# Attention on one core: score matmuls of 32 rows on a packed key tile, and the causal mask of the maximum pass added in PSUM by a matmul

## What is computed

```
scores = jnp.einsum('bhqd,bhkd->bhqk', q, k)
causal = jnp.tril(jnp.ones((t, t), bool))
scores = jnp.where(causal, scores, -jnp.inf)
attn = jax.nn.softmax(scores / np.sqrt(HEAD_DIM).astype(np.float32), axis=-1)
ctx = jnp.einsum('bhqk,bhkd->bhqd', attn, v)
```

## Time and profile before

| what | before |
|---|---|
| median of 3 runs | 1316.02 us (1314.12 to 1316.12) |
| span of the profiled execution | 1311.0 us |
| PE / DVE / ACT / POOL busy | 1194.1 / 1044.4 / 723.5 / 66.6 us |
| units L1204, score matmuls L1164, values L1184 | 1280, 1280 and 2560 matmuls |
| maxima L1314 and L1320 on VectorE | 768 and 512 |

### The profile page before, as it was taken

How to read it: one execution, slowest core, us unless ns; L and a number is a source line. 1 busy time by engine, 2 the same in 40 slices (tenths; PEclk the granted TensorE clock), 3 DMA queues, 4 the chain that set the end, 5 groups by cost and what they waited for, 6 DMA issues and landing times.

```text
span 1311.0 us, 21446 instructions
## 1 busy us (share of the span) xinstructions
PE 1194.1 (91%) x7781; PEld 510.1 (39%) x7781; DVE 1044.4 (80%) x3015; ACT 723.5 (55%) x861; POOL 66.6 (5%) x64
## 2 busy tenths in 40 slices
PE   1999958999999999999699979599999999999997
PEld 1455533333333333334455537233333333333336
DVE  8976588999999887875447567799999989878764
ACT  1322115566777777777332224156667777777773
POOL 5111010000000000000101000100000000000000
PEclk9999979999999999999799989799999999999999
DMA  4100142000000000000000000510000000000001
GB/s 147 34 1 1 39 131 58 2 1 2 2 1 1 2 1 2 1 1 2 1 0 1 1 1 25 154 48 2 2 1 2 2 1 1 2 1 2 2 2 33
DMA packets 23510, 23.26 MB, mean 18 GB/s; under 512 B 3134, under 2 KB 21220, under 8 KB 23404
## 3 DMA queue, kind: packets, MB, share of 16 engines
q1 hardware_dynamic: 22252, 18.73, 4.9%
q0 software_dynamic: 1152, 3.15, 0.9%
HBM read 13.20 MB, written 8.39 MB: 16 GB/s over the span
## 4 chain that ended last, share of the span: by engine, by line
PE 70%; DVE 22%; issue 4%; ACT 2%; DMA 1%; SPq 0%; DVEq 0%; ACTq 0%
PE psum L1184 18%; PE psum L1204 17%; PE psum L1164 14%; PE psum L442 9%; DVE part_max L1314 8%; PE psum L466 2%; PE psum L903 2%; PE psum L1171 2%; DVE junk L1320 2%; DVE xn L167 1%; DVE norm_v L150 1%; PE psum L1224 1%; PE psum L918 1%; DVE norm_stats L141 1%; PE psum L427 1%
## 5 line engine op out<-in xcount | busy, mean ns | idle before, releaser
L1275 ACT ACTIVATE hidden<-psum,exp_scale 128x1024 f32<-128x1024 f32 (+3 forms) x640 | 597.7, 984 | 258.9 <-PE psum L1164 137.3
L1314 DVE TENSOR_REDUCE part_max<-psum 128x1 f32<-128x512 f32 x768 | 492.1, 686 | 59.1 <-PE psum L1204 53.9
L1204 PE MATMUL psum<-k_slots,q_slots 128*128 128x512 f16 (+3 forms) x1280 | 401.2, 356 | 34.2 <-DVE part_max L1314 12.2
L1164 PE MATMUL psum<-q_slots,k_slots 128*128 128x512 f16 (+3 forms) x1280 | 330.9, 348 | 6.3 <-ACT hidden L1275 3.5
L1184 PE MATMUL psum<-hidden,v_aug 128*9 128x512 f32 (+3 forms) x2560 | 293.7, 531 | 0.1
L1320 DVE CUSTOM_DVE_ANT_0 junk<-psum,causal_add 128x384 bf16<-128x384 f32 (+3 forms) x512 | 230.6, 488 | 49.0 <-PE psum L1204 45.9
L1204 PEld LDWEIGHTS psum<-k_slots,q_slots 128*128 128x128 f16 x1280 | 114.5, 97 | 361.1 <-DVE part_max L1314 177.5
L442 PE MATMUL psum<-parts,w_parts 128*128 128x512 f16 x768 | 180.4, 387 | 1.9 <-DVE parts L843 1.9
L1164 PEld LDWEIGHTS psum<-q_slots,k_slots 128*128 128x128 f16 x1280 | 118.3, 98 | 97.8 <-ACT hidden L1275 13.9
L442 PEld LDWEIGHTS psum<-parts,w_parts 128*128 128x128 f16 x768 | 73.7, 99 | 83.1 <-issue 6.8
L586 ACT CAST parts<-psum 128x512 f16<-128x512 f32 x64 | 37.2, 588 | 107.2 <-PE psum L427 107.2
(11 more groups left out here) (170 smaller groups left out, 730.5 us busy)
## 6 DMA issues: line engine op xcount, KB each, us to landing
q_slots<-q_rows SPq DMA_DIRECT2D x8, 512.0 KB, 3.7
k_slots<-k_rows POOLq DMA_DIRECT2D x24, 128.0 KB, 4.1
q_rows<-parts SPq DMA_DIRECT2D x18, 128.0 KB, 2.7
k_rows<-parts SPq DMA_DIRECT2D x18, 128.0 KB, 2.4
q_slots<-in_L_ffn_W_dram SPq DMA_DIRECT2D x2, 1024.0 KB, 6.5
k_slots<-k_rows SPq DMA_DIRECT2D x8, 128.0 KB, 3.9
q_slots<-nm_parts SPq DMA_DIRECT2D x64, 4.0 KB
out_dram<-x_res SPq DMA_DIRECT2D x4, 256.0 KB, 2.3
```

The lines of the kernel that those rows point to most:

```text
L1164: last = pe.matmul(psum[:, S_BANKS + 2 * (tile % 2) + par, off:CH], k_slots[:, G * g + 2 * pr + par, j * P:(j + 1) * P], q_slots[:, g, c * ...
L1204: last = pe.matmul(psum[:, bank, 0:w], q_slots[:, g, qb * P:(qb + 1) * P], k_slots[:, G * g + h, kc * CH:kc * CH + w], start=True, stop=True)
L1275: act.activation(probs[:, tile % NP, :, off:CH], psum[:, bank:bank + 2, off:CH], ACT.Exp, scale=exp_scale[:, layer:layer + 1]).then_inc(ex ...
L1314: dve.tensor_reduce(dst, psum[:, bank, :], axis=AX.X, op=ALU.max).then_inc(ring_read, 1)
```

## The change

1. `k_slots` is packed like `q_slots`: [128, 4, 2048], four heads in the 128 rows, no zeros beside them. Score matmuls and units use the 32 rows of their head alone (`rows_of(h)`), in both operands.
2. VectorE takes plain maxima of all units. The mask of a diagonal unit is added in PSUM by a matmul of `later_keys` and `ident_bf` (128 x 128 rows and columns) on the unit's last 128 columns (`mask_of`). `ring_items` takes a stretch of ring items in groups of at most three: scores of the diagonal units first, then their masks, and only a mask counts up `ring_full`. In a layer there are 170 such groups: 14 in the opening (8 of them of three units), 100 in turns with a full quad (8 of three), 56 in turns with a quad on the diagonal (2 of three).
3. `causal_add` and `junk` are gone. Keys are loaded by one DMA for a chunk, not four. POOL clears one plane of `k_slots` in place of the whole tile.

The masks of the score pass (now L1165) stay matmuls of 128 rows.

```diff
-        k_slots = sb("k_slots", [P, H, T], F16)
+        k_slots = sb("k_slots", [P, NG, T], F16)
...
-                    pool.memset(k_slots[:, :, :].rearrange("p h t -> p (h t)").bitcast(I32), 0).then_inc(slots_set, 1)
-                    pool.wait_ge(slots_set, 1)
+                    pool.memset(k_slots[:, 1, :].bitcast(I32), 0).then_inc(slots_set, 1)
...
-            def load_k_rows(engine, n, h):
+            def load_rows(engine, slots, m, n):
 
                 cols = slice(n * CH, (n + 1) * CH)
-                return engine.dma_start(k_slots[SLOT * h:SLOT * (h + 1), h::G, cols],
-                                        slot_dram[1].rearrange("(g h) i d t -> h (i d) g t", h=G)[h, :, :, cols])
+                return engine.dma_start(slots[:, :, cols],
+                                        slot_dram[m].rearrange("(g h) i d t -> (h i d) g t", h=G)[:, :, cols])
+
+            def rows_of(h):
+                return slice(SLOT * h, SLOT * (h + 1))
...
                     for par in range(2):
+                        rows = rows_of(2 * pr + par)
                         last = pe.matmul(psum[:, S_BANKS + 2 * (tile % 2) + par, off:CH],
-                                         k_slots[:, G * g + 2 * pr + par, j * P:(j + 1) * P],
-                                         q_slots[:, g, c * CH + off:(c + 1) * CH],
+                                         k_slots[rows, g, j * P:(j + 1) * P],
+                                         q_slots[rows, g, c * CH + off:(c + 1) * CH],
                                          start=True, stop=q not in diagonal)
...
-                        last = pe.matmul(psum[:, bank, 0:w], q_slots[:, g, qb * P:(qb + 1) * P],
-                                         k_slots[:, G * g + h, kc * CH:kc * CH + w], start=True, stop=True)
+                        last = pe.matmul(psum[:, bank, 0:w], q_slots[rows_of(h), g, qb * P:(qb + 1) * P],
+                                         k_slots[rows_of(h), g, kc * CH:kc * CH + w], start=True, stop=kc < c)
+                        if kc == c:
+                            return
...
+                def mask_of(item):
+
+                    (_, c), i, kc, _ = item[1]
+                    pe.matmul(psum[:, RING_BANKS + ring_no[item] % RING, i * P:(i + 1) * P], later_keys[:, :],
+                              ident_bf[:, :], start=False, stop=True).then_inc(ring_full, 1)
+
+                def ring_items(items):
+
+                    for first in range(0, len(items), RING):
+                        some = items[first:first + RING]
+                        masked = []
+                        for item in some:
+                            on_diagonal = item[0] == "scores" and item[1][2] == item[1][0][1]
+                            if not on_diagonal:
+                                for before in masked:
+                                    mask_of(before)
+                                masked = []
+                            ring_item(item)
+                            if on_diagonal:
+                                masked.append(item)
+                        for item in masked:
+                            mask_of(item)
...
-                                dve.tensor_tensor_reduce(out=junk[:, n % 2, 0:w], in0=psum[:, bank, 0:w],
-                                                         in1=causal_add[:, CH - w:CH], scale=1.0,
-                                                         scalar=-3.0e38, op0=ALU.add, op1=ALU.max,
-                                                         accum_out=dst).then_inc(ring_read, 1)
-                                junk_used[n % 2] = n + 1
+                            w = CH if kc < s[1] else (i + 1) * P
+                            dve.tensor_reduce(dst, psum[:, bank, 0:w], axis=AX.X, op=ALU.max).then_inc(ring_read, 1)
...
-                    for h in range(G):
-                        load_k_rows(pool, proj.order[n], h).then_inc(k_landed[proj.order[n] - 1], 16)
+                    load_rows(pool, k_slots, 1, proj.order[n]).then_inc(k_landed[proj.order[n] - 1], 16)
...
-                        for h in range(G):
-                            load_k_rows(sp, c, h).then_inc(q_landed[c], 16)
+                        load_rows(sp, k_slots, 1, c).then_inc(q_landed[c], 16)
```

More of the change, by code:

```diff
@@ L1248, in _ @@
                         score_tile(q, 0)
[L1249 to L1250 removed]
+                    ring_items(items[cuts[0]:cuts[1]])
                     if q:
                         score_tile(q, 1)
[L1253 to L1254 removed]
+                    ring_items(items[cuts[1]:cuts[2]])
                     if previous:
                         values(previous)
[L1257 to L1258 removed]
+                    ring_items(items[cuts[2]:cuts[3]])
                     previous = q
```

34 lines of the change are left out of this document (6 added, 28 removed).

## The result

| what | before | after |
|---|---|---|
| median | 1315.89 us (1314.12 to 1316.12, 4 runs) | 1432.88 us (1427.92 to 1443.11, 4 runs) |
| ratio | 1 | 1.0909, 95% interval 1.0862 to 1.0956 |
| the profiled execution: time, span | span 1311.0 us | 1427.92 us, span 1426.0 us |
| mean granted clock of the span | 0.975 | 0.850 |
| time at half clock, 2 x (1 - clock) x span | 66 us | 428 us |

What follows compares the result with a forecast made beforehand. PE was taken to bound plain turns, VectorE only 0.23 us behind. Terms summed to +10.3 us a layer, +20.6 for both, less 1.5 for loads: +19 on 1316, so 1335 us, range 1303 to 1366.

Steps and rivals of the forecast that it cites:

- The granted clock is taken as now.: Whole kernel: the forecast time assumed PE's granted clock stays as in the profile before, 1.00 in the attention stretches.
- The rival that named it: Granted clock falls to half over a tenth of 320 turns because of small PE stops: +48 us, 1383 us; chance 0.04.
- A change of shape: PE switching between matmuls of different rows x columns: 0.096 us each, 550 more changes, 53 us of PE a layer.
- the rival of a cheaper change: Changes to 32-row tiles cost less than priced, deciding at 0.077 us; at 0.055 the kernel is faster, 1290 us; chance 0.22.
- the serial one: Rival: 32-row tiles run one after the other, so the pairs save nothing: 1448 us; chance 0.06.
- Item 2: Turns with a full quad and no diagonal unit (41 a layer): side-by-side pairs save 9.1 us a layer.
- Item 5: Turns with a quad on the diagonal and diagonal units (31 a layer): +11 us a layer, between 0 and 17.8.
- Item 3: Turns with a full quad and diagonal units (55 a layer): pairs against shape changes and masks, +3 us a layer.
- Item 4: Turns with a quad on the diagonal, no diagonal unit (33 a layer): +1 us a layer, between -4 and +5.5.
- Item 1, the opening: Opening of 32 diagonal units: VectorE idles 0.48 to 0.63 us before masks in eight groups of three, +4.4 us a layer.
- "0" for the smaller clearing: POOL's smaller clearing of the key tile (13.7 us before) was priced at 0, as nothing waits for it.
- VectorE's gain from the masks, 0: VectorE's plain maxima in place of masked reads: next to no gain, since the next read hides the difference; 0 us.

Runs made afterwards that it cites:

- run 3: Kernel before, with 32-row matmuls in the score pass alone (padded key tile, masks on VectorE, units at 128 rows): 1327.56 us, ratio 1.010.
- run 4: Kernel before, with 32-row matmuls in the units alone (padded key tile, masks on VectorE, score tiles at 128 rows): 1375.21 us, ratio 1.046.
- run 5: Kernel before, with 64-row score pairs and units everywhere, heads paired across halves, padded key tile, masks on VectorE: 1315.3 us, ratio 1.0013.
- run 8: The change with 64-row tiles in place of 32, padded key tile, unit masks on PE: 1384.78 us, ratio 1.056 to the kernel before.
- run 9: Kernel before, with 64-row score pairs and units only in turns whose quad is off the diagonal, masks on VectorE: 1286.24 us, ratio 0.9785.
- run 7: The changed kernel with every unit matmul issued twice: 1605.51 us, ratio 1.218 to the kernel before.
- run 10: Kernel before, with 32-row score pairs and units only in turns whose quad is off the diagonal, masks on VectorE: 1326.10 us, ratio 1.008.
- run 2: Kernel before, with unit masks on PE in groups of up to three, all matmuls of 128 rows, padded key tile: 1352.17 us, ratio 1.029.
- run 12: Kernel before, with unit masks on PE, each right behind its unit, all matmuls of 128 rows: 1330.14 us, ratio 1.012.
- run 14: Kernel before, with the key tile's clearing cut into 16 pieces and placed behind the first norm: 1305.63 us, ratio 0.993.
- run 1: The change with its unit masks back on VectorE, 32-row matmuls and packed key tile kept: 1370.99 us, ratio 1.030 to the kernel before.
- run 11: Kernel before, with 64-row score work only in turns off the diagonal and unit masks on PE in groups: 1342.34 us, ratio 1.022.
- run 13: Kernel before, with the key tile's clearing cut into 16 pieces at the same place: 1314.10 us, ratio 1.0001.

## Why the prediction was wrong

**"The granted clock is taken as now."** This is the step that failed. The rival that named it had a chance of 0.04 and a size of "a tenth of 320 turns". Its cost per turn was about right: 1.5 us predicted, and (51.8 - 0.8) x 2 = 102 us over the 80 turns with half clock in the change are 1.3 each. But it struck 80 of 318 turns, a quarter, and the range stopped short of it. I had asked only whether PE would stop more often. In the traces the large losses, 170 to 440 us of half clock beyond the 66 of before, come only where units and pairs both have 32 rows, with PE's records covering 97% of the time in the stretch shown; the loss is 19 to 110 us when either kind has 128 rows (runs 3, 4) or both have 64 (runs 5, 8, 9), and twice the 32-row streaming does not bring it back (run 7). The Trainium skill (TensorE: Matmul & The Clock Gate, What's actually happening) says that the clock follows how busy PE has been; measured here, a PE busy by its records is not enough. So the rows of the tiles are shown to be a cause, and why they are is not: "too little of the array" is a name for it, and how rows, columns and zeros count is open. Nor are 32 rows enough for the loss. The 63 turns from ((0,3),0) on ran at 0.98 in the first layer of the change and 0.93 in the second, in run 10 at 1.00 and 0.96, and nothing here tells why those held and the steps before them did not.

**The sum without the clock.** Its large terms held. A change of shape: 0.096 predicted; above, the two masks from 360.47 end their streams at 360.58, and the values step starts at 360.69, 0.11; a 384-column unit from 360.21 ends at 360.37 and the mask starts at 360.47, 0.10. So the price of the rival of a cheaper change (under 0.077) is refuted, and so is the serial one. Most pairs start 0.003 to 0.004 us apart, below even the lower bound of 0.007; I had taken 0.03. Item 2: -9.1 and -8.3. Item 5: +11 and +9.1. Item 3 was +3 and came to -2.8: more overlap of units with pairs than I took would do that, and is the other half of that rival, but no run tests it alone. Item 4: +1 and +2.8, inside its bounds. Together +0.8 a layer at full clock for +5.9.

**Item 1, the opening.** +4.4 a layer for the groups of three. With 128 rows (run 2) first unit to first values step took 39.44 us in the first layer (31.47 before) and 40.35 in the second (31.00 before): +8.0 and +9.4, part of it half clock. Ungrouped (run 12), the second layer's opening is back at 23.89 us to its first score pair. The mechanism was right; the term was put at half of what it is. In the change the openings cost +11.4 and +11.6, some 3 a layer more than in run 2: the clock there is lower (0.60 and 0.58 to the first values step, 0.78 and 0.63 in run 2), and 27 more changes of shape stand in each opening, of which item 1 priced only one for each group of three. The two are not told apart.

**"0" for the smaller clearing.** Wrong by 9 us (run 14) to 12 (the first unit of the change). I had counted only who waits for POOL's semaphore, and nobody did; the hold shows as busy time of VectorE, 11.64 us for four columns in the row of L150.

**Loads, -1.5.** From the issue of the queries' load to the first unit are 857.38 - 851.64 = 5.74 us, 6.18 before: -0.4.

**VectorE's gain from the masks, 0.** Its busy time fell by 15 us, and no time came of it: giving the masks back to it gains 62 us (run 1 against the change, by the medians of all executions) and 56 (run 9 against 11).

The account, between the spans: ahead of the first unit -11.6, openings +23.0, turns at full clock +1.6, turns at half clock +102.1, between the layers -2.0, behind them +1.9; together +115.0. Without the fall of the clock the change would have ended near 1316 - 12 + 17 + 2 = 1323, an estimate that takes the openings of run 2 (with those of the change it is 1329). That is inside the range, and partly by luck: the turns came 10 us under their term and the openings 9 over it, which cancels, and the 12 us of the clearing were not in the sum at all.

## What to carry to other kernels

Row tiles side by side do save PE time (2.81 to 2.47 us in the plain turn here), but check the granted clock of the stretch where all score work runs in them: 64-row tiles with zeros beside the head kept most of the clock that 32-row tiles lost, and won 2.2% where they stood only in turns off the diagonal (run 9); used everywhere (run 5) they won nothing. Keep full rows where other full-row matmuls stand between, since each change of shape cost 0.10 us here. And look for a short VectorE instruction with a long record before calling GpSimd's work free.

## What the runs showed that I had not expected

- The granted clock stood at 0.51 for 100 us while PE's records covered 97% of it. A microsecond of half clock costs about a third of a microsecond here: between two executions of the change, 1443.11 - 1427.92 = 15 us for some 48 us more of it (clocks 0.835 and 0.850).
- Masks that "fit in PE's slack" cost 38 us in 128 rows (run 2, against 1313.85) and 15 ungrouped (run 12, against 1314.82).
- A VectorE instruction of four columns was held for 12.38 us, over fourteen GpSimd clearings of 0.9 us each (run 13), much as for 11.64 us by one of 13.75.
